# C of the scan pass of layer 2: one load per span spread by ACT, or eight loads per half

## The reference, cut to what matters

```python
def step(state, inp):
    d, b, c, uu = inp
    dA = jnp.exp(d[..., None] * A_neg[:, None, :, :])
    state = dA * state + (d * uu)[..., None] * b[:, :, None, :]
    y = jnp.einsum('kbcn,kbn->kbc', state, c)
    return (state, y)
```

## Time and profile before

| | |
|---|---|
| median of 3 runs | 18105.77 us |
| profiled execution | 18079.56 us, its span 18077.9 us |
| mean granted TensorE clock | 0.818 of full speed |
| PE / PEld busy | 14837.0 us (82%) / 10962.3 us (61%) |
| DVE / ACT / POOL busy | 11267.9 us (62%) / 7510.9 us (42%) / 6783.4 us (38%) |
| DMA | 2640.24 MB, 1692803 packets, mean 146 GB/s |
| scan pass (layer 2) | first load at 8511.63 us, last scan at 16437.74 us |

### The profile page before, as it was taken

How to read it: one execution, slowest core, us unless ns; L and a number is a source line. 1 busy time by engine, 2 the same in 40 slices (tenths; PEclk the granted TensorE clock), 3 DMA queues, 4 the chain that set the end, 5 groups by cost and what they waited for, 6 DMA issues and landing times. The chain is left out here.

```text
span 18077.9 us, 359613 instructions
## 1 busy us (share of the span) xinstructions
PE 14837.0 (82%) x130080; PEld 10962.3 (61%) x130080; DVE 11267.9 (62%) x10440; ACT 7510.9 (42%) x12873; POOL 6783.4 (38%) x3199
## 2 busy tenths in 40 slices
PE   7899997999989745444888888888888888888899
PEld 5666665666666412222767767776777667765467
DVE  5666666666666555554777766766777667765532
ACT  4444444444444354444444444444444444442200
POOL 1000000000000042334777767766777667773100
PEclk9999998999999877776777777777777777777799
DMA  5222222222222276668889999999999999998711
GB/s 118 67 60 59 56 56 68 56 56 62 56 67 51 87 182 151 160 163 203 209 209 211 209 209 208 208 206 208 210 210 210 209 209 210 210 209 213 218 37 43
DMA packets 1692803, 2640.24 MB, mean 146 GB/s; under 512 B 1081676, under 2 KB 1245260, under 8 KB 1667404
## 3 DMA queue, kind: packets, MB, share of 16 engines
q1 hardware_dynamic: 1645388, 2493.45, 58.5%
q0 software_dynamic: 12288, 86.71, 2.2%
q10 hardware_dynamic: 34944, 57.81, 1.1%
HBM read 2110.03 MB, written 556.32 MB: 147 GB/s over the span
## 5 line engine op out<-in xcount | busy, mean ns | idle before, releaser
L1713 DVE TENSOR_TENSOR_SCAN L2.h<-L2.ps,L2.db 128x912 f32<-128x912 f32 x2688 | 5514.7, 2056 | 2415.4 <-POOL L2.db L1578 2311.1
L1578 POOL TENSOR_TENSOR L2.db<-L2.du,L2.bt 128x896 f32<-128x896 f32 x2688 | 5582.1, 2095 | 2395.1 <-DMA L2.du<-du 2298.4
L1601 PE MATMUL L2.ps<-L2.dm,L2.wa 32*128 32x112 f32 (+2 forms) x24192 | 4480.3, 343 | 1176.2 <-DVE L2.h L1713 1045.2
L1601 PEld LDWEIGHTS L2.ps<-L2.dm,L2.wa 32*128 32x128 f32 x24192 | 4123.2, 255 | 1889.1 <-DVE L2.h L1713 1352.2
L1653 ACT ACTIVATE L2.ps<-L2.ps 128x896 f32<-128x896 f32 x2688 | 2425.9, 902 | 4603.0 <-PE L2.ps L1601 4601.7
L1613 PE MATMUL L2.ps<-L2.h,L2.cd 128*8 128x96 f32 x50176 | 2575.9, 362 | 4.2 <-DVE L2.h L1713 4.2
L1613 PEld LDWEIGHTS L2.ps<-L2.h,L2.cd 128*8 128x8 f32 x50176 | 1441.3, 108 | 584.4 <-DVE L2.h L1713 4.3
L314 POOL TENSOR_TENSOR L1.x_res<-L1.x_res,L1.ob 96x3136 f32 (+1 forms) x16 | 95.4, 5976 | 2582.4 <-ACT L1.qv L457 2582.4
L366 PE MATMUL L0.p_proj<-L0.xt,L0.w_hi 128*96 128x448 f32 x3024 | 825.8, 383 | 195.1 <-DVE L0.xt L560 168.5
L366 PE MATMUL L1.p_proj<-L1.xt,L1.w_hi 128*96 128x448 f32 x3024 | 826.1, 383 | 194.4 <-DVE L1.xt L560 167.8
L314 POOL TENSOR_TENSOR L0.x_res<-L0.x_res,L0.ob 96x3136 f32 (+1 forms) x16 | 95.8, 6006 | 2369.5 <-ACT L0.qv L457 2369.5
(11 more groups left out here) (255 smaller groups left out, 19228.5 us busy)
## 6 DMA issues: line engine op xcount, KB each, us to landing
L2.du<-du SPq DMA_DIRECT2D x2688, 448.0 KB, 11.1
L2.dm<-d SPq DMA_DIRECT2D x896, 336.0 KB, 11.0
y<-L2.ysum SPq DMA_DIRECT2D x896, 84.0 KB
L0.left<-table SPq DMA_DIRECT2D x48, 1176.0 KB
L0.right<-table SPq DMA_DIRECT2D x48, 1176.0 KB
L1.left<-table SPq DMA_DIRECT2D x48, 1176.0 KB
L1.right<-table SPq DMA_DIRECT2D x48, 1176.0 KB
du<-L2p.work SPq DMA_DIRECT2D x64, 784.0 KB, 7.6
```

Of the source, the lines that this page charges most:

```text
L1578: pool.tensor_tensor(db[:, n % RB, :, 2:ROW], du[:, n % RD, :].rearrange("p (c t) -> p c t", t=SPAN), row, ALU.mult)\
L1601: mm = pe.matmul(decays[n % RA][:, a:b], wa[rows, j, :], dm[rows, j, a - lo:b - lo], start=True, stop=True)
L1713: dve.tensor_tensor_scan(h[:, half, u * UNIT:(u + 1) * UNIT, :].rearrange("p c t -> p (c t)"), decays[n % RA], db[:, n % RB, :, :].rearran ...
```

## The change

`cd` loses its half: one block-diagonal C for a span, used by the sums of both halves. SP loads C of all images into a plain tile `cc` (128 x 112) with one transfer, at u = 3 of the first half only, once ACT has read the `cc` before (`cd_made`). ACT makes `cd` from it after the last unit of the first half: eight activations (Identity with a scale for each partition), one for each image b, that multiply all 128 rows by a column of a 0/1 mask `image`. It waits for `cc` and for the sums of the span before, which read the old `cd`. The sums of the second half's turn (those of the first half's states) wait for `cd_made`; the waits on `cd_in` go. The mask is an input that is loaded once, and the memset of `cd` goes.

```diff
-        cd = m.sb("cd", [128, 2, BATCH, SPAN])
+        cc = m.sb("cc", [128, SPAN])
+        cd = m.sb("cd", [128, BATCH, SPAN])
+        image = m.sb("image", [128, BATCH])
...
-            def load_cd(k, s, half):
-                for b in range(BATCH):
-                    sp.dma_start(cd[STATES * b:STATES * (b + 1), half, b, :], bc_dram[1, k, b, :, span_of(s)]).then_inc(cd_in[half], 16)
+            def load_cc(k, s):
+                sp.dma_start(cc[:], bc_dram[1, k].rearrange("b n t -> (b n) t")[:, span_of(s)]).then_inc(cc_in, 16)
...
-                    if u == 3:
-                        if not (isinstance(fills, int) and fills == 0):
-                            sp.wait_ge(sum_ready, fills)
+                    if u == 3 and half == 0:
+                        made = count(sp, k, s, BATCH)
+                        if not (isinstance(made, int) and made == 0):
+                            sp.wait_ge(cd_made, made)
                         steady(sp)
-                        load_cd(k, s, half)
+                        load_cc(k, s)
...
             sp.wait_ge(cleared, 1)
+            sp.dma_start(image[:], ap["c_image"]).then_inc(image_in, 16)
...
-                        mm = pe.matmul(ps[32 * q:32 * q + BATCH, bank, i * HALF:(i + 1) * HALF], cd[:, half, :, t],
+                        mm = pe.matmul(ps[32 * q:32 * q + BATCH, bank, i * HALF:(i + 1) * HALF], cd[:, :, t],
                                        h[:, half, :, 2 + t], start=True, stop=True)
...
-                            pe.wait_ge(cd_in[1 - half], count(pe, k, s, 128, 128 * half))
+                            if half:
+                                pe.wait_ge(cd_made, count(pe, k, s, BATCH, BATCH))
...
+            act.wait_ge(image_in, 16)
+
+            def make_cd(k, s, fills):
+
+                act.wait_ge(cc_in, count(act, k, s, 16, 16))
+                act.wait_ge(sum_ready, fills + 2 * FILLS)
+                for b in range(BATCH):
+                    act.activation(cd[:, b, :], cc[:], ACT.Identity, scale=image[:, b:b + 1]).then_inc(cd_made, 1)
...
+                if half == 0:
+                    make_cd(k, s, before)
...
-            dve.memset(cd[:], 0.0)
...
+    out["c_image"] = (p[:, None] // STATES == np.arange(BATCH)).astype(np.float32)
```

More of the change, by code:

```diff
@@ L1397, in _, with scan_layer @@
                     finish(pr, j)
-def scan_layer(nc, sems, tag, wa_dram, d_dram, du_dram, bc_dram, y_dram):
+def scan_layer(nc, sems, tag, ap, wa_dram, d_dram, du_dram, bc_dram, y_dram):
     m = Pool(nc, sems, tag)
@@ L1428, in scan_layer @@
         bt_in = [m.sem(f"bt_in{s}") for s in range(2)]
-        cd_in = [m.sem(f"cd_in{s}") for s in range(2)]
+        image_in = m.sem("image_in")
+        cc_in = m.sem("cc_in")
+        cd_made = m.sem("cd_made")
         du_in = [m.sem(f"du_in{s}") for s in range(RD)]
@@ L1639, in _ @@
             pe.wait_ge(scanned, DIRS * HALVES * UNITS + RB)
-            pe.wait_ge(cd_in[1], 128 * DIRS * NSPANS)
             for f in range(FILLS):
@@ L2139, in network @@
         prep_layer(nc, None, "L2p", x2, ap, z, xc, d, du, bc, consts)
-        scan_layer(nc, None, "L2", wa, d, du, bc, y)
+        scan_layer(nc, None, "L2", ap, wa, d, du, bc, y)
         fin_layer(nc, None, "L2f", x2, x3, ap, z, xc, y, consts)
```

## The result

The changed kernel takes 17657.15 us (median of 4 runs, 17644.26 to 17676.29) against 18103.49 us (also the median of 4): ratio 0.9755 (0.9738 to 0.9772), 446 us less. The forecast was 17545 us, 560 us less. The profiled execution has 17676.29 us, a span of 17674.6.

What follows compares the result with a forecast made beforehand. Bound: DMA queue filling, emptied each half by SP's cd issues. DMA gain of 650 us, limited by TensorE to 560: 18079.6 - 560 = 17520, plus 26 for the median = 17545 us; range 17170 to 17920.

Steps and rivals of the forecast that it cites:

- the last step of the sum: TensorE's clock-limited floor, 32.8 us a half, cuts the DMA gain of 650 us to 560 us.
- What bounds the kernel: Filling of the DMA queue: SP's eight cd issues, 5.2 us a half on average, leave it empty.
- The removed gap: DMA idle time around SP's cd issues: about 2.8 us a half, 2.9 with saved bytes, 650 us in all.
- What is late next: TensorE: In the scan pass, PE's floor of 32.8 us a half at mean clock 0.74 limits the gain to 560 us.
- The sign named for it: DVE's waits for ACT's decay grow from 34 us into the hundreds if PE takes over.
- Rival A: DMA gets all and PE's clock rises: 31.2 us a half, gain 920 us, 17185 us; chance 0.17.
- The y wait (rival B): On SP, cd issue time becomes waiting before the y stores: gain 224 us, 17880 us; chance 0.15.
- ACT at nothing: Eight added ACT instructions a span, 2.3 us, fit ACT's idle time without a table load; uncovered, up to 258 us.
- Bytes only (C): On the DMA queue, only the saved cd bytes count: gain 31 us, 18075 us; chance 0.05.
- slower (D): PE's clock stays low in every sum phase: 36.2 us a half, 190 us slower, 18300 us; chance 0.07.
- The signs: Empty DMA windows after y stores under 1 us, share near 0.96, POOL's du wait from 2211 to about 1650 us.

Runs made afterwards that it cites:

- aligned kernel: Changed kernel with the mask tile widened from 32 to 64 bytes a partition, so du starts at a multiple of 512 bytes: 17524 us, 0.9673 of before.
- later stores: Four y stores moved from behind unit 2's du load to unit 4's: 17628 us in the changed kernel, 17430 us with du at a multiple of 512 bytes.
- spread loads: Kernel before with the same eight cd loads of a half, one behind each du load of units 3 to 10: 17584 us, 0.9726 of before.

## Why the prediction was right, and where it was not

The time fell into the range and near the forecast, but the last step of the sum was wrong and a term was missing; that the two came out nearly even is luck.

- *What bounds the kernel:* right. The block of cd issues left the DMA queue empty; spreading the block in place of removing it gives the gain, putting it back takes the gain away.
- *The removed gap:* right. The term was 2.9 us a half, 650 us. The engines' idle time fell by 2.9 us a half, from 3.2 to 0.3. As time of the kernel, with du's start restored, it is 18102 - 17524 = 578 us, 2.6 us a half, a tenth less than the term.
- *The term that was missing:* the layout. I followed each instruction of the diff and not the tiles' sizes; du moved 32 bytes off a multiple of 64 and took back 133 us. The aligned kernel differs from the changed one in nothing but where the tiles behind the mask start.
- *"What is late next: TensorE":* wrong, as far as the runs show. It took the gain from 650 down to 560 us, and so nearer to 446, for a cause that didn't act: the DMA share reached 0.99, so it was the DMA engines that had no time left, and with half of the sums gone the gap between the two kernels stayed. The sign named for it went the other way: DVE's waits for the decay fell from 34.0 to 25.5 us. Those for the carry, which ACT runs behind the decay, grew from 49.3 to 166.4 us, but both together grew by 0.5 us a half only. What the long half at a clock of 0.66 and the short one at 0.83 show is that the halves differ with the level of the clock (35.63 and 30.53 us); that it sets the mean is not shown. (The sum of a unit costs 3.67 - 2.16 = 1.5 us in the rows shown, not 1.6; nothing hangs on it.)
- *Rival A* had the better account of what comes next: DMA gets all. The share did rise to 0.99, and the clock in part (0.74 to 0.77). Its 920 us stand for a queue at 1.03 and the old time for a byte, and neither came.
- *The y wait (rival B):* SP's waits for ACT grew from 596.1 to 702.4 us only. The later stores show its price: 69 to 95 us with du aligned.
- *ACT at nothing:* right within what the runs can tell. Eight take 2.34 us where 2.3 were computed, and no second table load was recorded. They don't always fit into the idle time: in the rows above the next decay stands right behind the masks, without a gap, 1.22 us after PE began its spread. The aligned kernel lies only 21 us above the one without masks and loads, and that holds the masks, the cc load and its bytes together.
- *Bytes only (C), slower (D):* refuted by the spread loads, and by a clock that rose. (C's 31 us are 0.17% of the time, not 0.14%.)
- *The signs:* the share came to 0.99 where 0.96 was named, POOL's wait for du to 1811.8 us where 1650 was; both show the slower queue. The hole behind the y stores is nearly gone in one half shown (0.90) and still 6 us at 0.61 in the other.

## What to carry to other kernels

Read the DMA share in windows of a few microseconds, beside the list of the queue that feeds it: a mean of 0.91 can be a full queue with a hole, and here a run of small issues between two large loads made the hole. Spread such a run before you think of removing it. When a change alters the size of any tile, work out where the tiles behind it now start, and compare DMA share over GB/s before and after.

## What was not expected of the hardware

- Loads of 3584 bytes a partition into a tile that starts 32 bytes off a multiple of 64 took 3.4 to 4% more DMA engine time for a byte (4.50 against 4.33 to 4.35), 133 and 166 us of these kernels; their packets took 245.6 and 247.5 ns in place of 235.4 to 237.2. With a start at a multiple of 64, but not of 512, it was 243.8 ns, and 45 us were left. Why is open. db moved with du, but no transfer touches it, and POOL's and DVE's instructions lasted the same (2095 and 2097 ns, 2056 ns).
- With half of the state sums left out, PE was granted 0.50 throughout the pass in both kernels, though it was busy for 6685.61 of 7200 us in one of them; with all sums, at 6349 of 7200, it had 0.77. Busy time as recorded does not by itself say which level is granted; at the lower level the same matmuls also count as busy for longer (2.16 against 1.21 us for a spread).
